# TensorE's table of work beside a sort, laid out with other prices; two chunks of an aggregation moved into the loop behind it

## What is computed

```python
h = relu(layernorm(x))
q, k, v = h @ Wq + bq, h @ Wk + bk, h @ Wv + bv      # 8 heads of 32
s = einsum('ehd,ehd->eh', q[src], k[dst])            # one row of 8 scores an edge
attn = softmax of s over the edges of one src
x = x + segment_sum(attn * v[dst], src) @ Wo + bo
h = relu(layernorm(x))
aggr = segment_sum(edge_attr_256, dst)               # 100,000 rows of 256
x = x + mlp(concat([h, aggr]))                       # W1, W2, W3
```

## Time and profile before

| | us |
|---|---|
| median of 3 runs | 2132.82 |
| lowest and highest of them | 2123.03, 2134.06 |
| the profiled execution's own time | 2143.54 |
| its span from the first to the last instruction | 2141.7 |

### The profile page before, as it was taken

The page is one execution under the profiler, slowest core; times in us unless marked ns, Lnnn a source line. Parts: engine busy times, 40 slices in busy tenths (PEclk is TensorE's granted clock), DMA queues, the critical chain, the costliest instruction groups (busy, mean ns, idle before and its releaser), DMA issues.

```text
span 2141.7 us, 26167 instructions
## 1 busy us (share of the span) xinstructions
PE 1582.1 (74%) x6793; PEld 1126.0 (53%) x6793; DVE 1410.9 (66%) x2316; ACT 921.1 (43%) x2765; POOL 1017.2 (47%) x1024
## 2 busy tenths in 40 slices
PE   4799986376677676767677666776766767789998
PEld 4545564254455454645455555554544544556664
DVE  9997875175566665666666566665655677866663
ACT  5544443264444454544444444454544300144442
POOL 5001068335565555555555565655655575342210
PEclk7799998598898887888887779888978876899999
DMA  7135267467787787878777788887877766443331
GB/s 190 40 109 182 96 227 217 122 210 246 244 274 249 251 271 246 264 256 266 251 240 239 236 261 261 268 257 249 271 234 253 224 209 184 145 121 112 105 98 35
DMA packets 237277, 439.78 MB, mean 205 GB/s; under 512 B 47021, under 2 KB 148042, under 8 KB 237120
## 3 DMA queue, kind: packets, MB, share of 16 engines
q0 software_dynamic: 72256, 216.77, 32.3%
q1 hardware_dynamic: 138408, 132.97, 19.2%
q10 hardware_dynamic: 26456, 88.28, 12.6%
HBM read 385.03 MB, written 72.44 MB: 214 GB/s over the span
## 4 chain that ended last, share of the span: by engine, by line
PE 33%; DVE 23%; issue 18%; another core or an unknown queue 16%; ACT 7%; POOL 2%; DMA 1%; DVEq 0%; ACTq 0%; POOLq 0%; SPq 0%
PE bank L1099 6%; DVE V L1714 6%; DVE V L1759 5%; PE bank L1199 4%; PE bank L1381 4%; DVE V L1718 3%; PE bank L1071 2%; ACT EBO L846 2%; ACT EBO L848 2%; PE bank L1402 2%; POOL EBO L693 2%; PE bank L1072 2%; PE bank L1390 2%; PE bank L1364 2%
## 5 line engine op out<-in xcount | busy, mean ns | idle before, releaser
L712 POOL DMA_INDIRECT U<-kv_rows,dstb x856 | 859.2, 1004 | 635.5 <-DVE V L1759 386.7
L1099 PE MATMUL bank<-EBO 128*128 128x256 f32 x1568 | 451.1, 434 | 309.1 <-ACT R L856 164.6
L1099 PEld LDWEIGHTS bank<-EBO 128*128 128x128 f32 x1568 | 330.9, 217 | 404.2 <-issue 341.5
L1199 PE MATMUL bank<-V 128*128 128x264 f32 x1712 | 485.7, 426 | 74.9 <-issue 47.5
L1199 PEld LDWEIGHTS bank<-V 128*128 128x128 f32 x1712 | 352.8, 210 | 183.2 <-issue 79.0
L1714 DVE TENSOR_TENSOR V<-U,bank_pair 128x1024 f32<-128x1024 f32 x214 | 259.3, 1212 | 246.4 <-issue 245.1
L848 ACT ACTIVATE EBO<-EBO,ones 128x128 f32<-128x128 f32 x709 | 284.8, 402 | 27.5 <-ACT EBO L846 3.4
L846 ACT ACTIVATE EBO<-iota,dA 128x128 f32<-128x128 f32 x709 | 278.9, 393 | 0.4 <-issue 0.2
L1759 DVE TENSOR_TENSOR V<-U,bank 128x1024 f32<-128x1024 f32 x214 | 259.7, 1213 | 0.0
L1718 DVE TENSOR_REDUCE V<-V 128x32 f32<-128x1024 f32 x142 | 173.3, 1220 | 4.9
L908 ACT ACTIVATE V<-V 128x32 f32<-128x32 f32 x142 | 35.7, 252 | 252.5 <-remote 195.0
(11 more groups left out here) (304 smaller groups left out, 2062.7 us busy)
## 6 DMA issues: line engine op xcount, KB each, us to landing
EBO<-in_edge_attr_dram ACTq DMA_DIRECT2D x163, 512.0 KB
V<-q_rows SPq DMA_DIRECT2D x128, 128.0 KB
EBO<-in_edge_attr_dram SPq DMA_DIRECT2D x31, 512.0 KB
o_log<-R SPq DMA_DIRECT2D x108, 132.0 KB
o_log<-V SPq DMA_DIRECT2D x106, 132.0 KB
U<-kv_rows,dstb POOLq DMA_INDIRECT x856
kv_rows<-U SPq DMA_DIRECT2D x49, 256.0 KB, 2.0
ag_rows<-R SPq DMA_DIRECT2D x98, 128.0 KB
```

Source lines behind the costliest of these rows:

```text
L712: e.indirect_dma_start(out=kvb[:, b % NKV, j, :], out_offset=None, in_=kv_dram[:, :], in_offset=bass.IndirectOffsetOnAxis(ap=dstb[:, k:k + ...
L1099: m = e.matmul(agg_bank(c)[:, 0:D], oh2[i][0:n, j, :], eb[h % NEB][0:n, j % 4, :], start=j == 0, stop=j == 7)
L1199: t = e.matmul(bank[3 + i][:, 0:RW], oho[i], PV[i][:, j, :, :].rearrange("p h d -> p (h d)"), start=j == 0, stop=j == 3)
```

## The change

One line of prices in the planner differs:

```diff
-        STG, TILE, STEP, TURN, BACK = 1.40, 3.5, 0.48, 1.4, 0.2
+        STG, TILE, STEP, TURN, BACK = 1.33, 3.3, 0.46, 1.4, -0.6
```

## The result

| | kernel before, us | kernel after, us |
|---|---|---|
| median, 20 runs each, same chip | 2124.11 | 2144.99 |
| lowest and highest | 2106.86, 2153.15 | 2121.07, 2161.01 |
| profiled execution, its own time | 2143.54 | 2149.18 |

The kernel after is slower: its ratio is 1.0083 with the 95% interval 1.0057 to 1.0109, some 18 us. The ratio leaves out executions more than 1.5% above the fastest of the same kernel, which is why its 18 us are a little less than the 20.9 between the medians. The forecast was 2133 and no measurable change; 2145 is still in the range, near the edge that rival 1 had set.

What follows compares the result with a forecast made beforehand. No single engine was taken to bound the kernel: TensorE comes late in the sort, a ring of waits holds the batches. Sort -3.0 and two chunks +3.1 gave +0.1 on the 2132.8 median: 2133 us, range 2121 to 2146.

Steps and rivals of the forecast that it cites:

- rival 1: Batches: chunk borders fall at worse places; three more borders holding the ring add 15 us, 2148; chance 0.17.
- the two chunks: Batches: two added chunks cost 1.5 us each, from the paces with and without aggregation; +3.1 us, bounds 0 and 8.2.
- The reading of the sort: Sort's second part: VectorE is ready and TensorE late, by 3.5 to 5.2 us; the end moves only with the last turns.
- Turns 1 to 4: Sort: a tile more makes turn 1 later by 3.7 us; turns 2 to 4 are later by 2.8 us.
- the walk: Turn-by-turn pricing of the sort's tiles, steps and one-hots; claimed the sort ends 3.0 us earlier.
- Turn 5: Sort: three tiles for four, TensorE's 12.0 us under VectorE's 14.6, so VectorE decides; start at 212.1.
- turn 15: Sort's last turn: 96 steps instead of 112, start 344.4 against 347.38; gain 3.0 us, or 2.1 at the lower clock.
- The five first steps: Sort, behind turn 11: five steps at 0.65 us each, ending at 288.9, +1.3 us.
- GpSimd: Sort: third chunk's one-hots start at 291.1, 4.1 us later, at 0.93 us each; done by about 343.
- Turn 14: Sort: 76 steps instead of 83 ahead; one-hots 3.7 us less but 4.1 later, so +0.4: start at 329.7.
- Rival 3: Batches: the added chunks' transfers are the price, +8.2 us, total 2138; chance 0.12.
- Rival 4: Sort: turn 1's 3.7 us are not won back, the end stays within 1 us; 2136, chance 0.10.

Runs made afterwards that it cites:

- e2: Kernel after, but with 112 steps kept in the sort and the batches of before; against the kernel before on a quick chip: 1781.38 us, ratio 1.0039.
- e5: The kernel after itself, unchanged, as a control against the kernel before on a slow chip: 2152.09 us, ratio 1.0142.
- e12: The kernel after again, unchanged, against the kernel before on a quick chip: 1774.3 us, ratio 1.0008.
- e1: Kernel before with its sort cut to 96 steps, so 86 chunks in the batches; against the kernel before on a quick chip: 1770.02 us, ratio 0.9984.
- e4: Kernel before with 96 sort steps, 84 chunks where they were and two added behind them; quick chip: 1769.46 us, ratio 0.998 to before.
- e10: The same kernel as e4, run again against the kernel before on a quick chip: 1770.1 us, ratio 0.9984.
- e11: The same kernel as e4, run a third time against the kernel before on a quick chip: 1770.0 us, ratio 0.9982.
- e6: The same kernel as e1, run against the kernel before on a slow chip: 2140.03 us, ratio 1.006.
- e7: Kernel before with ScalarE copying a finished chunk out first in its batch; against the kernel before on a slow chip: 2154.36 us, ratio 1.0133.
- e8: Kernel before with no chunk starting in the third batch of a group of four; against the kernel before, slow chip: 2138.99 us, ratio 1.0056.
- e3: Kernel before with its 84 chunks started at the pace of 86; against the kernel before on a quick chip: 1775.03 us, ratio 1.0008.

## Why the prediction was wrong where it was

**The range held, the sum did not.** The sum was -3.0 for the sort and +3.1 for the two chunks. The sort gave 0, and what else changed cost some 18 us where the result was measured. The 2145 lies in 2121 to 2146 because the range had been stretched towards rival 1, whose mechanism was then not borne out; that the range held was luck.

**The reading of the sort** stood: TensorE is late for VectorE, and only the last turns count. In e2 the last turn comes straight behind the steps, with no idle time of TensorE, and 6.8 us of sort stand against 6.9 us of time.

**Turns 1 to 4** came as the walk had them, 0.9 to 1.0 us early all along (turns 1, 2 and 4: 168.74, 172.37, 196.50 against 169.70, 173.35, 197.4). In e5 and e2, with the same table, they came 0.7 to 0.9 us later than that, so this is scatter. VectorE's wait behind turn 1 was 7.38 us (forecast 8.4), and there is none worth naming ahead of turn 2.

**Turn 5 was mis-sized.** It started at 211.22, as walked (212.1), and VectorE decided it. But TensorE had been idle for 2.53 us, and then its eight transposes took 1.39 us instead of 1.04 and the L1071 behind them 2.00 instead of 1.12. The granted clock from 211.2 to 215.3, and for the next paragraph that of the first steps and of later ones:

```profile
211.20:215.30 4.10, 4.08 (x13) 2.35 (x14) 3.89 (x9) 0.37 (x1) 0.00 (x0) 0.58 0.01 4
286.50:290.60 4.10, 4.10 (x10) 3.29 (x11) 0.00 (x0) 0.00 (x0) 0.00 (x0) 0.53 0.81 303
299.40:301.90 2.50, 2.45 (x12) 2.17 (x13) 0.85 (x2) 0.45 (x2) 2.50 (x4) 1.00 0.78 221
```

0.58 of full speed, so most of it at 1.2 GHz; turn 6 came 9.97 us behind turn 5, not 0.87 + 2 x 3.72 = 8.3: 1.7 us. In e5, e12 and e2 it is 10.02, 9.97 and 9.99, so this is no accident of one execution. The Trainium skill, "TensorE: Matmul & The Clock Gate", Part 1, says that an idle array falls to the half rate; this row agrees. The prediction had weighed that price for turn 15 alone. At turn 15 (2.93 us idle) the transposes took 1.14 us, 0.1 more, and at turn 2 (2.59 us idle) 1.09: there the same rule would have cost too much. The walk put new pauses ahead of turns 2, 5 and 15 and priced the clock at one of them.

**The five first steps were mis-sized.** They took 290.65 - 286.50 = 4.15 us where the walk had 3.25; in e5, e12 and e2 it is 4.40, 4.32 and 4.29. The price of 0.65 was the mean of twenty records, of which the first ran at the low level and the rest don't; with only ten, at a granted clock of 0.53, only those at the low level are left. The same ten records take 2.40 us at 299.45, at 1.00. This is 0.9 us.

**GpSimd** then started the third chunk at 293.08 (forecast 291.1), took (28.23 + 7.41) / 36 = 0.99 us a one-hot (0.93) and stood 0.93 us for a buffer. So its start had moved by 6.0 us, from 287.03, and not by 4.1, and it finished its last one-hot at 348.4, where the prediction had about 343; before it was 348.3. Turn 14 came at 332.78 (329.7). VectorE from there needed 14.7 us, as walked. (The walk's 268.7 + 12.0 + 5.0 for the first steps is 285.7, not 285.8; this changes nothing.) The account: -0.9 at turn 5, +1.7 for its clock, +0.9 for the steps, +0.3 more until GpSimd starts and +1.1 until turn 14 make +3.1. The sort term was -3.0 and measured 0, by this trace and by the mean of three.

**The two chunks.** The sum had +3.1, bounds 0 and 8.2. On quick chips e1, e4, e10 and e11 are 0.16 to 0.20% faster, about 3 us, of which the sort explains 2.3 to 2.8, and the batches take as long with 86 chunks as with 84: the two chunks cost nothing that can be seen, the lower bound, and the reason named for it, gathers that hold the ring, fits. On slow chips e6 is 0.60% [0.2, 1.0] slower, 12.7 us, with a shorter sort: the two chunks and the places that the others take with them cost about 15 us. The kernel after, with no gain in the sort, has 18 us [12, 23] and 30 us [20, 40] there. This is the step that failed: the difference of two paces of one execution was taken for the price of a chunk. Of its +3.1 nothing shows on quick chips, and on slow chips the cost is five to ten times as large, where two kernels with the 84 chunks of before (e7, e8) lost as much.

**Rival 1** had the direction, the size (2148) and its mark in the trace, three more borders. Its mechanism was not borne out: e7 and e8 took a third and a quarter of that wait away and lost 1.3 and 0.6%, with 84 chunks and an untouched sort. That new places of the borders cost something by another way is not excluded. **Rival 3**: no chip charged for transfers: the quick one moves 333 GB/s at a DMA share of 0.96, and is not slower for the chunks, and the slow one stands at 0.79. **Rival 4** came true as to the sort, though 2.6 us of what was lost there were the clock's (1.7 + 0.9), which it did not name. **Rivals 2 and 5** didn't, on the chip of the result; rival 5's free chunk is the quick chips' case.

**What stays open.** All four other arrangements of ScalarE's and TensorE's work in the batches that ran on a slow chip were slower than before, by 0.6 to 1.4%, with 84 chunks or 86. So the amount is not needed for such a loss; whether in the kernel after it is the amount or the pace was not told apart, since e3 and e4 never ran on a slow chip. And what the "remote" waits wait for is not known: they are there on slow chips alone, in the stretch in which GpSimd issues gathers. That they are the cost is argued from this, not shown, and their sum does not follow the times: from 500 to 1600 us it is 469 us in before and 473 in after and in e8, 520 in e5, 536 in e7, 546 in e6.

**A version that beats both** on quick chips is e4: 0.9980, 0.9984 and 0.9982 on three chips, 3 us, about what the sort gains. e1, which spreads the 86 chunks evenly, does as well there (0.9984). Both keep the tiles where they were, and cut only the steps ahead of the last turn. On a slow chip e4 hasn't run, and e6 there is a warning.

## What to carry to other kernels

When work is moved off a late engine, look for every pause that this opens, and give the work behind each pause two prices, at the full and at the lower clock: here pauses of 2.5 to 2.9 us cost 1.7 us once and next to nothing twice. A mean over a run that begins slowly is too cheap for the few instructions that begin it. Where several engines hang in a ring of waits, the share of a wait, or the difference of two paces, is no price: undo or move one part and time it, since a wait that is cut may come back under another name. And before a change of half a per cent is believed, run it, with the kernel before beside it, on a second chip.

## What the runs showed of the hardware

- The kernel before took 2124 us on some chips and 1773 on others. The sort took the same time on both (the last turn at 347.5 us in the kernel after on either), and the batches did not: in the kernel after 6.8 against 5.2 us each, DMA 256 against 333 GB/s, granted clock 0.84 against 0.96.
- A pause of 2.53 us of TensorE ahead of turn 5 was followed by 4.1 us at 0.58 of the clock, which cost 1.7 us; in the three other executions with the table of after the stretch from turn 5 to turn 6 took as long to 0.05 us; 2.59 us ahead of turn 2 was followed by transposes of 1.09 us, next to nothing. After 8.11 us (e1) they took 1.97, nearly double.
- On the quick chips GpSimd issued a gather every 1.3 us (1.0 us of work, 0.3 between) and a batch of four took 5.20 us with the aggregation beside it and 5.26 without. On a slow chip the gathers lasted as long, 1.0 us each, and GpSimd waited 264.5 of 1100 us for buffers.
